# Slot placement moved behind a transposition of the sums, and part of the rotations and of the tile names moved from VectorE to GpSimd

## What is computed

```python
def _L0_attn_ref(x, W_q, W_k, W_v, W_o):        # H = 16 heads of DK = 8
    Q = apply_rope(proj(W_q), pos, inv_freq)
    K = apply_rope(proj(W_k), pos, inv_freq)
    V = proj(W_v)
    scores = jnp.einsum('bhqd,bhkd->bhqk', Q, K) / jnp.sqrt(jnp.float32(DK))
    attn = jax.nn.softmax(scores, axis=-1)
    out = jnp.einsum('bhqk,bhkd->bhqd', attn, V)
    return out.transpose(0, 2, 1, 3).reshape(b, s, D) @ W_o.T
def _L0_ffn_ref(x, Wg, gamma, beta, W1, b1, W2, b2):   # E = 8 experts, top 2, F = 512
    scores = xf @ Wg
    w, idx = jax.lax.top_k(scores, K)
    w = jax.nn.softmax(w, axis=-1)
    normed = xhat[None, :, :] * gamma[:, None, :] + beta[:, None, :]
    h = jax.nn.relu(jnp.einsum('end,edf->enf', normed, W1) + b1[:, None, :])
    out = jnp.einsum('enf,efd->end', h, W2) + b2[:, None, :] + xf[None, :, :]
    y = jnp.einsum('ne,end->nd', cw, out)
xn = _layernorm(x, axis=-1)
x = x + _L0_attn_ref(xn, ...) + _L0_ffn_ref(xn, ...)
```

## Time and profile before

| | |
|---|---|
| three runs | 635.98, 635.57, 634.03 us (median 635.57) |
| the profiled execution | 635.57 us, of which the span of its records 633.7 us |
| TensorE busy (matmuls) | 567.0 us, 89% of the span |
| ScalarE busy | 502.9 us, 79% |
| VectorE busy | 371.8 us, 59% |
| GpSimd busy | 211.7 us, 33% |
| mean granted TensorE clock | 0.981 of full speed |

### The profile page before, as it was taken

The page is one execution under the profiler, slowest core; times in us unless marked ns, Lnnn a source line. Parts: engine busy times, 40 slices in busy tenths (PEclk is TensorE's granted clock), DMA queues, the critical chain, the costliest instruction groups (busy, mean ns, idle before and its releaser), DMA issues.

```text
span 633.7 us, 12156 instructions
## 1 busy us (share of the span) xinstructions
PE 567.0 (89%) x4620; PEld 239.3 (38%) x4620; DVE 371.8 (59%) x1109; ACT 502.9 (79%) x552; POOL 211.7 (33%) x267
## 2 busy tenths in 40 slices
PE   8899658978999999988999999998899999989774
PEld 6233102213445444434345444443444444444111
DVE  4966786787545554677564545466765445444482
ACT  3699749967878888777877878887787888878993
POOL 4399600024665323232332332322333233321000
PEclk9999969988999999999999999999999999999997
DMA  6167301001110202000220110200022011120620
GB/s 238 31 184 223 101 0 35 1 18 43 34 40 26 57 25 59 18 21 15 55 60 21 27 53 25 60 18 17 22 56 60 18 41 44 21 56 13 268 103 35
DMA packets 25361, 35.47 MB, mean 56 GB/s; under 512 B 5440, under 2 KB 15728, under 8 KB 24784
## 3 DMA queue, kind: packets, MB, share of 16 engines
q1 hardware_dynamic: 19936, 23.70, 12.2%
q0 software_dynamic: 4544, 9.32, 5.4%
q10 hardware_dynamic: 816, 1.61, 0.7%
HBM read 17.36 MB, written 8.85 MB: 41 GB/s over the span
## 4 chain that ended last, share of the span: by engine, by line
PE 60%; DVE 19%; ACT 14%; issue 4%; DMA 2%; ACTq 1%; DVEq 0%; another core or an unknown queue 0%
PE acc L628 24%; ACT ring L841 14%; PE aside_bank L672 11%; PE sc L594 9%; PE aside_bank L682 9%; DVE work L1223 3%; PE aside_bank L661 3%; PE aside_bank L521 2%; DVE blocks L1010 2%; DMA sin<-rope_sin 2%; PE aside_bank L691 2%; DVE xn L1212 2%; DVE rotated L883 1%; DVE turned L1189 1%; PE aside_bank L505 1%
## 5 line engine op out<-in xcount | busy, mean ns | idle before, releaser
L841 ACT ACTIVATE ring<-sc 128x1024 f32<-128x1024 f32 x512 | 489.0, 1044 | 105.3 <-PE sc L594 89.2
L628 PE MATMUL acc<-ring,v 128*9 128x512 f32 x2048 | 271.2, 602 | 32.7 <-DVE blocks L1010 16.5
L449 POOL DMA_INDIRECT work<-normed,token x71 | 70.4, 992 | 313.0 <-DVE work L1217 251.1
L1223 DVE TENSOR_SCALAR work<-aside_bank,xn 128x128 f32<-128x128 f32 x284 | 79.9, 344 | 110.3 <-PE aside_bank L672 103.8
L594 PEld LDWEIGHTS sc<-qs,ks 32*128 32x128 f16 x1024 | 26.0, 91 | 229.3 <-ACT ring L841 179.7
L594 PE MATMUL sc<-qs,ks 32*128 32x512 f16 x1024 | 102.2, 388 | 4.4 <-ACT ring L841 1.9
L672 PE MATMUL aside_bank<-work,xn 128*128 128x128 f32 x568 | 82.4, 288 | 7.0 <-DVE work L1217 5.9
L459 POOL DMA_INDIRECT token_out<-work,token x71 | 71.8, 1011 | 42.6 <-DVE work L1217 19.5
L672 PEld LDWEIGHTS aside_bank<-work,xn 128*128 128x128 f32 x568 | 69.2, 192 | 23.7 <-issue 23.7
L682 PE MATMUL aside_bank<-xn,work 128*128 128x128 f32 x568 | 75.1, 275 | 0.0
L682 PEld LDWEIGHTS aside_bank<-xn,work 128*128 128x128 f32 x568 | 71.4, 196 | 0.3 <-DVE work L1223 0.3
(11 more groups left out here) (184 smaller groups left out, 328.1 us busy)
## 6 DMA issues: line engine op xcount, KB each, us to landing
w_all<-L_ffn_W SPq DMA_DIRECT2D x16, 256.0 KB, 4.6
qs<-hl SPq DMA_DIRECT2D x60, 64.0 KB
ks<-hl SPq DMA_DIRECT2D x60, 64.0 KB
x<-L_attn_x SPq DMA_DIRECT2D x4, 512.0 KB, 7.9
normed<-xn SPq DMA_DIRECT2D x4, 512.0 KB, 3.2
xn<-token_out SPq DMA_DIRECT2D x2, 1024.0 KB, 5.8
w_all<-token_out SPq DMA_DIRECT2D x2, 1024.0 KB, 11.0
out<-x SPq DMA_DIRECT2D x8, 256.0 KB, 2.2
```

The costliest lines, as they stand in the source:

```text
L449: pool.indirect_dma_start(out=xt[t % TILE_BUFFERS], out_offset=None, in_=xh_d[:, :], in_offset=bass.IndirectOffsetOnAxis(ap=token[:, 0, t: ...
L628: last = nc.tensor.matmul(acc[32 * j:32 * j + VW, :], v9[:, b, kb, 4 * g + j, :], ring[:, (2 * n + j // 2) % UNITS, j % 2, :], start=(kb = ...
L841: nc.scalar.activation(ring[:, (2 * n + u) % UNITS, :, :], sc[score_pair(2 * n + u)][:, :].rearrange("p (h c) -> p h c", h=2), ACT.Exp, sc ...
L1223: last = nc.vector.tensor_scalar(hT[t % 2][:, c, :], bank[0][:, c * P:(c + 1) * P], w_tile[t % 3][:, B1_AT + c:B1_AT + c + 1], 0.0, ALU.ad ...
```

## The change

- Tables: the slots are placed at step 24, behind `tail(2)`, with the ranks, which were at step 22; the expert rows' transposition (`COLUMNS_AT`) goes from 25 to 22; the top choices of a batch are made in two halves at two steps. Marks 0 and 1 are at steps 27 and 28, the others each at the step of an inversion; the inversions are at 33, 35, 36, 38, 39, 41, 42 and 44; `tokens` at 45; the first tile at 47; experts from step 48. The rotations of batch 1 are at 37, 43, 46 and 50, those of the later batches at 36, 41, 45 and 50 of a batch.
- GpSimd makes `named` (two instructions a group, 16 in all) and waits for `mark_ok`; TensorE's `invert` waits for `named_ok` too. `tile_mark` gets a second buffer.
- `split` moves to GpSimd, without the sine product: add, copy to float16 and difference (3 instructions for each of 12 pieces). The first stands before the first gather, the others in given rounds of the tile loop (`SPLIT_ROUND`). VectorE keeps the sine product (`take_sine`), one step after the piece or, among the experts, at the next step of `SECOND`, behind the tile's rows. `rotated` gets three buffers.

```diff
-WO_AT, COLUMNS_AT = 3, 25
+WO_AT, COLUMNS_AT = 3, 22
-TOP_AT = {4: 0, 11: 1, 16: 2, 20: 3}
+TOP_AT = {4: (0, 0), 5: (0, 1), 11: (1, 0), 12: (1, 1), 17: (2, 0), 18: (2, 1), 20: (3, 0), 21: (3, 1)}
-ROUTE_AT, RANKS_AT, SLOTS_AT, GATES_AT = 21, 22, 23, 26
+ROUTE_AT, RANKS_AT, SLOTS_AT, GATES_AT = 21, 24, 24, 26
-FFN_FROM, FFN_TO = 53, 237
+FFN_FROM, FFN_TO = 48, 237
...
+SINE_AT = {}
+for n, (b, r) in PLAIN_AT.items():
+    SINE_AT[n + 1 if n < FFN_FROM else min(m for m in SECOND if m > n and m % KB != KB - 1)] = (b, r)
+SQUARE_AT = {n + 3: piece for n, piece in SINE_AT.items() if piece[0] > 1}
+SQUARE_AT.update({n: (1, r) for r, n in enumerate((50, 51, 53, 55))})
+LAST_STEP = {t: n for n, t in SECOND.items()}
+SPLIT_ROUND = {piece: -1 if piece == (1, 0) else 3 if n < FFN_FROM else 5 + min(t for t in LAST_STEP if LAST_STEP[t] >= n)
+               for n, piece in SINE_AT.items()}
...
+            for g in range(GROUPS):
+                k, js = g % 2, slice(GROUP * g, GROUP * (g + 1))
+                pool.wait_ge(mark_ok, g + 1)
+                nc.gpsimd.tensor_scalar(named[k][:, :, 0, :], tile_mark[k], row_name, None, ALU.mult
+                                        ).then_inc(named_ok, 1)
+                nc.gpsimd.tensor_tensor(named[k][:, :, 1, :], tile_mark[k],
+                                        pick_name[:, js].unsqueeze(2).to_broadcast([P, GROUP, SLOT_TILES]), ALU.mult
+                                        ).then_inc(named_ok, 1)
+            def split(b, r):
+                c, s = ROPE_ORDER[r]
+                at = slice(c * CH, (c + 1) * CH)
+                pool.wait_ge(sine_ok, 4 * (b - 1) + r + 1)
+                nc.gpsimd.tensor_tensor(turned[r][:, :], turned[r][:, :], rotated[r % 3][:, :], ALU.add).then_inc(sum_ok, 1)
+                pool.wait_ge(sum_ok, 4 * (b - 1) + r + 1)
+                for k in range(2):
+                    pool.wait_ge(stack_in[k], loads_into(k, 2 * b))
+                pool.wait_ge(later_q_in, 16 * COPIES)
+                after(nc.gpsimd.tensor_copy(hl[:, s, 0, at], turned[r][:, :]))
+                nc.gpsimd.tensor_tensor(hl[:, s, 1, at], turned[r][:, :], hl[:, s, 0, at], ALU.subtract
+                                        ).then_inc(low_ok, 1)
+            split(1, 0)
             pool.wait_ge(ws_ok, 1)
-            pool.wait_ge(xh_out, 16 * B)
             pool.wait_ge(token_ok, 1)
...
+                for piece, split_round in SPLIT_ROUND.items():
+                    if t == split_round:
+                        split(*piece)
...
             def invert(g):
                 pe.wait_ge(mark_ok, g + 1)
+                pe.wait_ge(named_ok, 2 * (g + 1))
...
             def take_plain(b, r):
                 bank_is_full(0, "plain", b, r)
+                v.wait_ge(low_ok, 4 * b - 1)
                 times(turned[r][:, :], bank[0], r, cos)
-                nc.vector.stream_shuffle(rotated[:, :], bank[0], SWAPPED).then_inc(bank_taken[0], 1)
+                if r == 3:
+                    v.wait_ge(sum_ok, 4 * (b - 1) + 1)
+                nc.vector.stream_shuffle(rotated[r % 3][:, :], bank[0], SWAPPED).then_inc(bank_taken[0], 1)
+            def take_sine(b, r):
                 v.wait_ge(bank_taken[0], USE["plain", b, r])
-                link(times(rotated[:, :], rotated[:, :], r, sin))
+                times(rotated[r % 3][:, :], rotated[r % 3][:, :], r, sin).then_inc(sine_ok, 1)
```

More of the change, by code:

```diff
@@ L84 @@
 PROJECT_AT[STEPS - 4] = (B - 1, 0)
-FFN_FROM, FFN_TO = 53, 237
+FFN_FROM, FFN_TO = 48, 237
+NORM_AT = {PER_BATCH * b - 8: b for b in range(1, B)}
+FLAG_AT = {PER_BATCH * b - 6: b for b in range(1, B)}
 TAKEN = [n for at in (PLAIN_AT, NORM_AT, FLAG_AT, PROJECT_AT) for n in at]
@@ L178, in build @@
                       for k in range(2)]
-        tile_mark = marks[:, 2 * GROUP * P:2 * GROUP * P + GROUP * SLOT_TILES].rearrange("p (i c) -> p i c", i=GROUP)
-        named_at = 3 * GROUP * P
+        tile_at, named_at = 2 * GROUP * P, 2 * GROUP * (P + SLOT_TILES)
+        tile_mark = [marks[:, tile_at + k * GROUP * SLOT_TILES:tile_at + (k + 1) * GROUP * SLOT_TILES]
+                     .rearrange("p (i c) -> p i c", i=GROUP) for k in range(2)]
         named = [marks[:, named_at + k * 2 * GROUP * SLOT_TILES:named_at + (k + 1) * 2 * GROUP * SLOT_TILES]
@@ L192, in build @@
         turned = [sb(f"turned{k}", [P, CH]) for k in range(4)]
-        rotated = sb("rotated", [P, CH])
+        rotated = [sb(f"rotated{k}", [P, CH]) for k in range(3)]
         cos, sin = sb("cos", [P, S]), sb("sin", [P, S])
@@ L974, in _ @@
             v.wait_ge(bank_taken[0], USE["plain", 0, 2])
[L975 removed]
+            link(nc.vector.tensor_tensor(turned[2][:, :], turned[2][:, :], rotated[2][:, :], ALU.add))
             split_high(2).then_inc(high_ok, 1)
```

66 lines of the change are left out of this document (24 added, 42 removed).

## The result

The kernel after takes 650.38 us (median of 4 runs, 647.17 to 655.58), the kernel before, on the same chip, 635.54 us: a ratio of 1.0249 with a 95% interval of 1.0215 to 1.0284. It is **slower by 2.5%**, where 623.0 us were forecast and 635 was the upper end of the range. The profiled execution took 650.07 us with a span of 648.2 us, against 635.57 and 633.7 before.

What follows compares the result with a forecast made beforehand. TensorE was taken to bound steps with expert pieces, ScalarE's exponentials pure attention steps. Followed through the stages, step 237 starts at 575.5 instead of 588.0 us: -12.5 on 635.57, giving 623.0 us; range 613 to 635.

Steps and rivals of the forecast that it cites:

- Starting five steps earlier removes no work: Experts, steps 49 to 237: 142 pieces cost 0.45 us each over a free step anywhere; steps 64 to 237 take 407.2 us.
- the slower one: Rival, steps 34 to 46: GpSimd's names become the bound, 6.2 us a group, sum +5.1, 640.7 us; chance 0.08.
- Up to step 34: Front: waits at steps 24 and 26 go, `tail(3)` at step 32 waits 3.7 us; step 34 starts at 92.9, -9.9 us.
- The names: Steps 34 to 46: GpSimd's names take 4.0 us a group (3.2 alone); step 46 starts at 122.7, leaving -2.4 us.
- The Trainium skill's 1.03 cycles an element: Support for the quick-names rival, steps 34 to 46: first name about 0.7 us; sum -20.3, 615.3 us; chance 0.25.
- First tile: Tokens and first gather: gather no longer covered, a wait of some 2 us; step 49 starts at 130.3 us.
- The rotations' waits: Rotations of batches 2 and 3 among the experts: waits for columns mostly go, 3.5 us a batch, -7.0 us.
- The port among the experts: Expert steps: GpSimd's splits meeting VectorE's weight copies add 1 us.
- What follows step 237 is untouched: End of the kernel after step 237: length stays as before, no change.

Runs made afterwards that it cites:

- the one with the copy behind: Kernel after, pieces unmoved, but weight copies of steps 8k-1 issued at step 8k behind the sums' transposition: 637.12 us, ratio 1.0041 to the kernel before.
- the one from step 48 with both edits: Kernel after with splits of batches 2 and 3 back on VectorE and weight copies of steps 8k-1 behind the transposition: 646.89 us, ratio 1.0187 to the kernel before.

## Why the prediction was wrong

**The step that failed** is "Starting five steps earlier removes no work: the same 142 pieces cost 0.45 us each over a free step wherever they stand". They don't. A piece costs that where the step has slack; an empty step that follows a first piece and holds a transposition makes TensorE wait, 1.2 to 2.8 us in 14 of 15 cases, which the sum put at nothing. By the forecast's own points, the 27.1 us between 623.0 and 650.07 are: step 46 late by 1.8, the first tile by 0.9, steps 49 to 64 quicker by 0.5, steps 64 to 237 at 428.57 instead of 407.2 (+21.4), and the end +3.5. With the 13 pieces moved, steps 64 to 237 take 412.19 us: 16.4 of the 21.4 are these positions. The waits at the two that stayed are 4.7 more, which no run took out by themselves. The range failed with it, since no rival had a loss among the experts; the slower one stood at the names.

- *Up to step 34*: the mechanism is right, with a wait of 3.72 us for 3.7 at `tail(3)`. That the slots' place is a gain is shown from both sides (0.9926 alone, 1.0065 without it). That the number is so close, 92.84 for 92.9, is partly luck: step 26 came 1.0 us earlier than forecast, 0.66 of it ahead of the loop, and `weigh(32)` with the scores behind it took 1.0 us longer than forecast, at half the clock.
- *The names*: right in size, 4.14 us a group for 4.0, but not by the mechanism. The two instructions take 1.71 and 1.13 us undisturbed, 2.84 and not 3.2, and only two of the 16 took longer (3.20 and 2.15 us); the rest of the 4.14 is GpSimd waiting for marks. The step's reason for 4.0, that GpSimd's fixed parts and arithmetic need no port, is shown by no run. What the port cost fell mostly on VectorE's comparisons, 0.12 and 0.30 us each in the mean. The Trainium skill's 1.03 cycles an element (GPSIMD Engine Reference, section 3.1), some 0.7 us by an estimate, is not borne out: 1.71 us. Step 46 came 1.8 us late, and the names don't set it alone: the last inversion began 1.3 us after they were done. The working passed over the wait of 3.93 us at `tail(4)`; with that wait nearly gone an inversion waited 4.04 us for the names, so the two chains are about equally long.
- *First tile*: right, a wait of 2.09 us for the gather where some 2 were put.
- *The rotations' waits*, -7.0: the waits went, since TensorE's idle time before `layer_one` fell from 7.0 to 2.0 us in the whole execution, and all its idle time between steps 64 and 237 but that before `weigh` by 11.8 us. It was spent on the same engine. That the splits' move to GpSimd earns it is not shown: with experts from 53 it was worth nothing, with experts from 48 some 1.5%.
- *The port among the experts*, +1: the mean of the 71 weight copies rose from 0.760 to 0.883 us, 8.7 us of VectorE's time, most of it covered. An uncovered one, as at step 104, is worth 1.1 us and is part of the waits above.
- *"What follows step 237 is untouched"*: off by 3.5 us. The order of the work there is the old one. From step 248 to the end the traces of thirteen kernels show 25.4 to 26.8 us and one of these "issue" waits. Three show 29.3 to 29.8 us and two: the kernel after, the one with the copy behind, and the one from step 48 with both edits, which have all their pieces at the same steps. The run with only the positions moved has 26.8 us, so some 2.5 us of its gain lie here. What decides it stays open.

## What to carry to other kernels

When work is spread over steps by a rate, write out the pattern and lay it over every other period in the program. Here 142 in 189 is three in four, and the transposition that comes every eighth step met an empty step at 15 of 22 places. The same rate in another phase had no such place and was 3.0% faster; a start one step later had four and was 4% faster. An empty step isn't a free one: the work of a piece covers the way to another engine and back, so a piece belongs exactly where such a wait falls. And a total busy time says nothing of this; the idle time before one group, with its releaser, showed it at once.
